# Attention over heads: block-diagonal grids in halves of 64 rows, with fewer and larger strided transfers

## What is computed

```python
fq = jax.nn.elu(q) + 1.0                        # q, k, v: token, 16 heads, 16 numbers
fk = jax.nn.elu(k) + 1.0
kv = jnp.einsum('bhnd,bhne->bnde', fk, v)       # for each token 16 x 16, summed over heads
qkv = jnp.einsum('bhnd,bnde->bhne', fq, kv)
qk = jnp.einsum('bhnd,bnd->bhn', fq, fk.sum(axis=1))
attn = qkv / (qk[..., None] + 1e-06)
```

## Time and profile before

| | |
|---|---|
| median of three runs | 728.25 us (727.19, 728.25, 729.0) |
| profiled execution, span from first to last instruction | 726.3 us |
| TensorE busy | 670.9 us, 92% of the span |
| VectorE, ScalarE, GpSimd busy | 481.1, 420.1, 326.5 us |
| TensorE's granted clock | full in the middle stage, 0.977 in the mean |
| matmuls on keys and on queries | 34.5 and 34.6 us busy, 1024 each |

### The profile page before, as it was taken

How to read it: one execution, slowest core, us unless ns; L and a number is a source line. 1 busy time by engine, 2 the same in 40 slices (tenths; PEclk the granted TensorE clock), 3 DMA queues, 4 the chain that set the end, 5 groups by cost and what they waited for, 6 DMA issues and landing times.

```text
span 726.3 us, 17454 instructions
## 1 busy us (share of the span) xinstructions
PE 670.9 (92%) x6214; PEld 567.6 (78%) x6214; DVE 481.1 (66%) x1332; ACT 420.1 (58%) x841; POOL 326.5 (45%) x493
## 2 busy tenths in 40 slices
PE   7689999998777999999999999999999885999994
PEld 5449999975566788888888888888888663999994
DVE  7856757425688766767777768677676565777751
ACT  5755556502334767676767676766754642766660
POOL 5234563122232453545573664745547563353312
PEclk9879999999999999999999999999999998999998
DMA  8479788404656444544555555555433343567720
GB/s 264 149 241 322 229 270 276 139 29 119 98 99 109 91 66 90 95 87 66 101 86 85 117 84 129 68 108 91 86 73 96 116 132 109 167 215 217 219 93 29
DMA packets 287104, 95.56 MB, mean 132 GB/s; under 512 B 213989, under 2 KB 284737, under 8 KB 287019
## 3 DMA queue, kind: packets, MB, share of 16 engines
q1 hardware_dynamic: 272298, 85.48, 48.9%
q0 software_dynamic: 3840, 8.32, 3.6%
q10 hardware_dynamic: 10880, 0.66, 1.0%
HBM read 65.09 MB, written 29.40 MB: 130 GB/s over the span
## 4 chain that ended last, share of the span: by engine, by line
PE 75%; DVE 8%; issue 6%; ACT 4%; POOL 2%; DMA 2%; SPq 1%; ACTq 1%; POOLq 0%; DVEq 0%
PE bank L1735 68%; PE bank L1744 7%; DMA qkv_rows<-feats 1%; POOL hids L795 1%; SPq L373 1%; ACTq L373 1%; ACT hids L1038 1%; DMA x_all<-in_L_attn_q_x_dram 1%; ACT feats L1001 1%; POOL table L677 1%; ACT feats L999 0%; DVE kv_ L1679 0%; ACT ots L1063 0%; DVE sth L1687 0%; DVE att_ L1576 0%
## 5 line engine op out<-in xcount | busy, mean ns | idle before, releaser
L1735 PE MATMUL bank<-down_w,hids 128*128 128x256 f32 x768 | 105.8, 286 | 1.9 <-POOL hids L795 1.6
L1735 PE MATMUL bank<-hnts,up_w 128*128 128x512 f32 x384 | 104.4, 407 | 0.0
L795 POOL TENSOR_TENSOR hids<-hid,hids 128x512 fp32r<-128x512 f32 x64 | 83.1, 1298 | 41.0 <-ACT hids L1038 40.6
L1735 PEld LDWEIGHTS bank<-down_w,hids 128*128 128x128 f32 x768 | 95.7, 188 | 6.2 <-POOL hids L795 3.4
L1735 PE MATMUL bank<-qkv_w,xnts 128*128 128x256 f32 (+1 forms) x384 | 76.4, 346 | 5.7 <-DVE xnts L1589 4.8
L1735 PEld LDWEIGHTS bank<-hnts,up_w 128*128 128x128 f32 x384 | 67.5, 189 | 11.4
L1735 PEld LDWEIGHTS bank<-qkv_w,xnts 128*128 128x128 f32 x384 | 60.6, 189 | 18.2 <-DVE xnts L1589 7.5
L1035 ACT ACTIVATE hid<-bank,cols 128x512 f32<-128x512 f32 x64 | 44.1, 688 | 45.8 <-PE bank L1735 45.5
L786 POOL TENSOR_SCALAR sth<-sth 128x1 f32<-128x1 f32 x32 | 7.2, 226 | 125.3 <-DVE sth L1601 125.3
L1735 PE MATMUL bank<-a_w,xa_h 128*128 128x256 f32 x256 | 60.2, 379 | 0.0
L1735 PE MATMUL bank<-xa_xt,a_w 128*128 128x256 f32 x384 | 55.1, 294 | 1.4 <-DVE xa_xt L1327 1.4
(11 more groups left out here) (272 smaller groups left out, 1546.9 us busy)
## 6 DMA issues: line engine op xcount, KB each, us to landing
qkv_rows<-feats SPq DMA_DIRECT2D x32, 384.0 KB, 3.4
a_raw<-in_L_ffn_w_dram SPq DMA_DIRECT2D x32, 256.0 KB, 4.1
a_w<-in_L_ffn_w_dram SPq DMA_DIRECT2D x32, 256.0 KB, 3.7
b_raw<-in_L_ffn_w_dram SPq DMA_DIRECT2D x32, 256.0 KB, 3.2
b_w<-in_L_ffn_w_dram SPq DMA_DIRECT2D x32, 256.0 KB, 3.0
mid_rows<-x_all SPq DMA_DIRECT2D x8, 512.0 KB, 2.9
x<-mid_rows SPq DMA_DIRECT2D x32, 128.0 KB, 2.4
values<-qkv_rows SPq DMA_DIRECT2D x32, 128.0 KB, 2.9
```

Source lines behind the costliest of these rows:

```text
L795: pool.tensor_tensor(hids[1][u % 3][:], hid[u % 2][:], f32(hids[0][u % 3][:]), ALU.subtract).then_inc(s_hidl, 1)
L1735: return pe.matmul(dst, left, right, start=start, stop=stop, skip_group_check=True)
```

## The change

The grids of keys and queries become half as wide. Partition `4*(16r+h)+u` of set `s` holds token `8s+2u+r`: the even tokens stand in partitions 0 to 63, the odd ones in 64 to 127, each half block-diagonal over four tokens in 64 columns. Each call of `mm` becomes two with 64 rows and 64 columns, the second half's results in the next bank (KV). All eight banks are now one PSUM tensor, so that one view (`sums`) spans both. Values, keys and queries are loaded by four transfers each of every fourth partition: 12 a tile. For every tile ScalarE's queue issues two of the keys and one of the queries (three for tile 0), SyncE the others. Copy and transpose read the new order. Bank KV holds a half of the sums, so `turn_o` moves to bank TURN, and the router's second turns and counts to bank V, with the waits that go with them.

```diff
+    HALVES, QUADS = 2, 4
+    HALF = P // HALVES
...
-        bank = [ctx.enter_context(nc.psum_tensor(f"bank{i}", [P, 512], F32)) for i in range(8)]
+        banks = ctx.enter_context(nc.psum_tensor("bank", [P, 8, 512], F32))
+        bank = [banks[:, i] for i in range(8)]
...
-            keys = tiles(mid, "keys_", 2, [P, SETS, P])
-            queries = tiles(mid, "queries_", 2, [P, SETS, P])
+            keys = tiles(mid, "keys_", 2, [P, SETS, HALF])
+            queries = tiles(mid, "queries_", 2, [P, SETS, HALF])
+            tile(mid, "below_x", [P, 2, SETS, P])
...
+        sums = banks[:, B_ATT:B_KV + 1, 0:4 * HALF]
...
-        HELPED = 7
+        HELPED = NT
         def keys_by_sp(n):
-            return (4 if n == 0 else 5) if n < HELPED else 8
+            return 2 if n < HELPED else QUADS
         def queries_by_sp(n):
-            return (2 if n == 0 else 6) if n < HELPED else 8
...
-        def issue_keys(engine, n, t):
...
-            i, rows = n % 2, slice(n * P, (n + 1) * P)
-            engine.dma_start(keys[i][t * HEADS:(t + 1) * HEADS, :, t * HD:(t + 1) * HD],
-                             qkv_rows[1, rows, :].rearrange(
-                                 "(s t) (h d) -> t h s d", t=8, h=HEADS)[t]).then_inc(s_kvin[i], 16)
...
-        def issue_queries(engine, n, t):
-            i, rows = n % 2, slice(n * P, (n + 1) * P)
-            engine.dma_start(queries[i][t * HD:(t + 1) * HD, :, t * HEADS:(t + 1) * HEADS],
-                             qkv_rows[0, rows, :].rearrange(
-                                 "(s t) (d h) -> t d s h", t=8, d=HD)[t]).then_inc(s_qin[i], 16)
+            return (1 if n == 0 else 3) if n < HELPED else QUADS
...
+        def of_quad(c, n, u):
...
+            return qkv_rows[c, n * P:(n + 1) * P, :].rearrange("(s u r) (k x) -> u (r k) s x", u=QUADS, r=HALVES, k=16)[u]
...
+        def issue_values(engine, n, u):
+            engine.dma_start(values[n % 2][u::QUADS, :, 0:HD], of_quad(2, n, u)).then_inc(s_kvin[n % 2], 16)
...
+        def issue_keys(engine, n, u):
+            engine.dma_start(keys[n % 2][u::QUADS, :, u * HD:(u + 1) * HD], of_quad(1, n, u)).then_inc(s_kvin[n % 2], 16)
...
+        def issue_queries(engine, n, u):
+            engine.dma_start(queries[n % 2][u::QUADS, :, u * HEADS:(u + 1) * HEADS], of_quad(0, n, u)).then_inc(s_qin[n % 2], 16)
         def set_of(i, j):
...
-                i, rows = n % 2, slice(n * P, (n + 1) * P)
+                i = n % 2
...
-                sp.dma_start(values[i][:, :, 0:HD], qkv_rows[2, rows, :].rearrange(
-                    "(s t) (g e) -> (t g) s e", t=8, g=HEADS)).then_inc(s_kvin[i], 16)
-                for t in range(keys_by_sp(n)):
-                    issue_keys(sp, n, t)
+                for u in range(QUADS):
+                    issue_values(sp, n, u)
+                for u in range(keys_by_sp(n)):
+                    issue_keys(sp, n, u)
             def load_queries(n):
...
-                for t in range(queries_by_sp(n)):
-                    issue_queries(sp, n, t)
+                for u in range(queries_by_sp(n)):
+                    issue_queries(sp, n, u)
             def store_x2(g):
...
-                for t in range(queries_by_sp(n), 8):
-                    issue_queries(act, n, t)
+                for u in range(queries_by_sp(n), QUADS):
+                    issue_queries(act, n, u)
             def help_keys(n):
...
-                for t in range(keys_by_sp(n), 8):
-                    issue_keys(act, n, t)
+                for u in range(keys_by_sp(n), QUADS):
+                    issue_keys(act, n, u)
             def copy_kvt(n):
...
-                act.copy(kvt[:], bank[B_ATT][:].rearrange("p (i c) -> p i c", i=4)).then_inc(s_kvt, 1)
+                act.copy(kvt[:].rearrange("p i (r d u) -> p i r d u", r=HALVES, d=HD),
+                         sums.rearrange("p r (i u d) -> p i r d u", i=4, u=QUADS)).then_inc(s_kvt, 1)
             def gelus(g, m):
...
-                    act.copy(ots[0][n % 2][:], bank[B_KV][:, 0:D]).then_inc(s_o, 1)
+                    act.copy(ots[0][n % 2][:], bank[B_TURN][:, 0:D]).then_inc(s_o, 1)
...
-                    features(n, bank[B_KV])
+                    features(n, bank[B_V])
...
-                dve.tensor_tensor(ots[1][n % 2][:], bank[B_KV][:, 0:D], f32(ots[0][n % 2][:]), ALU.subtract).then_inc(s_ol, 1)
+                dve.tensor_tensor(ots[1][n % 2][:], bank[B_TURN][:, 0:D], f32(ots[0][n % 2][:]), ALU.subtract).then_inc(s_ol, 1)
             def attended(n):
...
-                dve.transpose(att[:], bank[B_ATT][:].rearrange("p (i t h) -> p h i t", i=4, t=8)).then_inc(s_att, 1)
+                dve.transpose(att[:], sums.rearrange("p r (t h) -> p h t r", h=HEADS)).then_inc(s_att, 1)
...
-                    read_counts(routed(s, 2), bank[B_KV])
+                    read_counts(routed(s, 2), bank[B_V])
...
-                pe.wait_ge(s_kvin[n % 2], 16 * 9 * (n // 2 + 1))
+                pe.wait_ge(s_kvin[n % 2], 16 * 2 * QUADS * (n // 2 + 1))
...
-                        last = mm(bank[B_ATT][32 * j:32 * j + 32, i * P:(i + 1) * P], values[n % 2][:, set_of(i, j)],
-                                  keys[n % 2][:, set_of(i, j)], True, True)
+                        for r in range(HALVES):
+                            rows = slice(r * HALF, (r + 1) * HALF)
+                            last = mm(sums[32 * j:32 * j + 32, r, i * HALF:(i + 1) * HALF],
+                                      values[n % 2][rows, set_of(i, j)], keys[n % 2][rows, set_of(i, j)], True, True)
...
-                pe.wait_ge(s_qin[n % 2], 16 * 8 * (n // 2 + 1))
+                pe.wait_ge(s_qin[n % 2], 16 * QUADS * (n // 2 + 1))
...
-                        last = mm(bank[B_ATT][32 * j:32 * j + 32, i * P:(i + 1) * P], kv[:, i, 32 * j:32 * j + 32],
-                                  queries[n % 2][:, set_of(i, j)], True, True)
+                        for r in range(HALVES):
+                            rows = slice(r * HALF, (r + 1) * HALF)
+                            last = mm(sums[32 * j:32 * j + 32, r, i * HALF:(i + 1) * HALF],
+                                      kv[rows, i, 32 * j:32 * j + 32], queries[n % 2][rows, set_of(i, j)], True, True)
...
-                    last = turn(bank[B_KV][:, k * P:(k + 1) * P], on[n % 2][:, k * P:(k + 1) * P])
+                    last = turn(bank[B_TURN][:, k * P:(k + 1) * P], on[n % 2][:, k * P:(k + 1) * P])
...
-            kv_free = None
...
-                    pe.wait_ge(*kv_free)
+                    pe.wait_ge(*turn_free)
...
-                    kv_free = (s_ol, s - 4)
+                    turn_free = (s_ol, s - 4)
...
-                    if kv_free:
-                        pe.wait_ge(*kv_free)
...
-                    kv_free = (s_kv, s - 3)
...
-                    pe.wait_ge(*kv_free)
-                    turned(n, bank[B_KV])
-                    kv_free = (s_bfeat, n + 1)
+                    pe.wait_ge(*v_free)
+                    turned(n, bank[B_V])
+                    v_free = (s_bfeat, n + 1)
...
-                    pe.wait_ge(*kv_free)
-                    count(g, bank[B_KV])
-                    kv_free = (s_bdisp, 9 * g + 1)
+                    pe.wait_ge(*v_free)
+                    count(g, bank[B_V])
+                    v_free = (s_bdisp, 9 * g + 1)
...
-                    pe.wait_ge(*kv_free)
+                    pe.wait_ge(s_att, 4 * NT)
...

```

## The result

| | before | after |
|---|---|---|
| median of nine runs each, us | 729.19 (727.19 to 729.38) | 730.79 (730.32 to 732.34) |
| profiled execution, span, us | 726.3 | 729.9 |
| mean granted clock | 0.977 | 0.966 |

The ratio is 1.0031 (95% interval 1.0022 to 1.0039): slower by 0.3%, where 20 us less were forecast. The medians lie 1.6 us apart and the two profiled spans 3.5 us: the execution profiled before (728.25) is one of the faster of its nine, the one after (731.59) one of the slower. Ratios leave out executions over 1.5% above the fastest of the same kernel. In the page of the changed kernel the chain is as it was, TensorE's; the instructions fetched (q8) have grown from 50 packets of 0.82 MB to 66.

What follows compares the result with a forecast made beforehand. TensorE's stream was taken to bound the middle steps; 16.6 us there and in the last two tiles plus 3.4 in the first six steps made 20.0 off the 726.3 span, 706.3, plus 1.95: 708.3 us, range 702 to 722.

Steps and rivals of the forecast that it cites:

- The blocks: sum_kv and sum_att on TensorE: each block of matmuls takes 0.59 us instead of 1.01, 0.42 less, 0.84 a step.
- Rival 3: TensorE's blocks: doubled matmuls are handed out too slowly, 1.8 us a block, 775 us in total; chance 0.07.
- What ends next: Middle steps: ScalarE's copy of the values, which project needs, leaves 0.30 us spare; gains total 16.6 us.
- the 0.12 taken from 15 steps: Middle steps: part of sum_kv's 0.42 us lost to a new wait of project for the values' copy, leaving 0.72 a step.
- The wait for the choice of expert: Four middle steps where TensorE already waits 0.2 us for VectorE: wait grows to 0.6, all of sum_kv's 0.42 lost.
- ScalarE's issues: Three more transfers a tile on ScalarE's queue from the eighth tile on, covered by the table load: cost taken as 0.
- The first six steps: Steps from 181 to 234 us: fewer issues and shorter sum_att, less turn_o's delay, gain 3.4 us, bounds 0 and 7.
- The five gains of `sum_att`: Early steps: the shorter block on queries saves time five more times, 2.1 us in all.
- `turn_o`'s 0.2 us: Early steps: moved to bank TURN, it comes ahead of qkv in four or five steps, costing 0.9 us.
- The strided copies: ScalarE's copy of kvt reading PSUM at a step of 16 elements: taken as 0, at worst 0.50 us.
- Rival 1: ScalarE becomes the bound through a 0.50 us dearer strided copy or held-up issues: 12 us given back, 720; chance 0.14.
- rival 2: Halves of a column group take turns, or something other than columns sets the round: blocks stay 1.01 us, 727; chance 0.12.

## Why the prediction was wrong, point by point

**The blocks (mis-sized).** "64 recorded matmuls, eight side by side, again 8 rounds" of 0.055 us held for the first four rounds alone (0.238 us); the other four took 0.375 (0.32 with half the columns). A block gave 0.22 us, not 0.42; 10.7 us in 24 steps instead of 20. This is the largest term of the forecast, and it was sized at twice what came. Rival 3 had this mechanism, with its break-even of 16 ns a matmul: the rate was 11.7 ns, in half of the block, so it halved the gain and did not turn it. The row set against it, eight loads and four matmuls within 85 ns, showed the start of a block, where 32 stand ready; nothing in it could show the 33rd. The price set for this rival, 0.026 us a matmul, came from a row whose granted clock reads 0.50; the prediction did not say so. The 25 ns from start to start, which the prediction quoted from the Trainium skill ("TensorE: Matmul & The Clock Gate", section "Wait — 56ns, not 53.3ns?"), are contradicted in both parts of the block.

**What was not there at all: broken blocks.** They cost 3.8 us from tile 6 to tile 30 of the profiled run. Their cause is open. The run with the number of instructions of before (half of the sets, 50 packets fetched) has only two after its first two blocks, 0.58 and 0.19 us, but these first two lose 1.06 and 1.13, more than in the changed kernel (0.66 and 0.73); and the one with transfers to neighbouring partitions has the 66 packets and one broken block. That fetching instructions beside the grids' transfers breaks them is a guess that fits these two in part.

**What ends next (held).** ScalarE's chain keeps its distance from the block, so what is spare decides, and the block's gain was 0.22 us, less than the 0.30 that were spare: in the steps from 303 us on `project` starts as soon after `turn_kv` as before (0.35 us where nothing stands between), and the 0.12 taken from 15 steps did not come. In the four steps with 0.08 spare (256 to 291 us) it starts at 0.50 instead of 0.35: 0.15 lost, of a gain of 0.22, where 0.34 of 0.42 were predicted. The wait for the choice of expert grew from 0.2 to 0.4.

**ScalarE's issues ("Taken: 0").** In the middle this held for ScalarE's chain: they lay under the table load as predicted, and the relu came no later, though they took 0.58 to 0.66 us, not 0.31. What they cost in the total, 0.8 and 1.9 us by two pairs of medians, is not well told from nothing. The late turn of hn, 1.9 us in four steps, no step of the prediction foresaw; it comes with and without these issues, ScalarE's copy ahead of it waits for TensorE's own turn, and its cause is open. "Bytes and pieces of 64 bytes are the same" was true and beside the point: the step of partitions was not weighed.

**The first six steps (wrong sign).** +3.4 was forecast, -5.3 came. The largest part is the first tile: 1.5 us were to be won by fewer issues ahead of its copy of kvt, and tile 1's keys came 3.8 us later. The prediction counted the issues and left out what they wait for. ScalarE's keys of tile 1 wait for that tile's store, and SyncE issued the store 1.5 us later, behind the dearer transfers; so the copy came 1.9 us later instead of sooner, TensorE waited 3.1 us, and the clock fell. The five gains of `sum_att` did not exist: TensorE's next work there waits for VectorE's low part of hn, and that wait grew from 0.36 to 0.55 us. `turn_o`'s 0.2 us cost 0.94 in four or five steps, as said. The clock fell three times, at most 5.6 us, of which idle products gave back 2.8 by tile 5. No step of the prediction asked what fewer busy microseconds in an engine that waits do to its clock, though the stretch was known to be busy 41 of 53 us.

**The strided copies** cost nothing, as taken: the copy of kvt takes 0.587 us before and after. The transpose takes 0.708 instead of 0.704. Rival 1's price did not exist; rival 2's mechanism neither.

**The rest.** After tile 30, 1.05 us were lost. Kernels with the same last stage lie between 185.4 and 187.2 us there (before 185.8, after 186.9), so this is no effect of the change that these runs can show.

The sum, from tile 6 to tile 30: 10.7 from the blocks and 0.3 at `turn_o`, less 3.8 of broken blocks, less 2.0 between `project` and the turn of hn, less 2.4 elsewhere (0.6 in the projection of queries, keys and values with the wait for the choice behind it, 0.6 in the router's logits, 0.5 in its counts, 0.4 ahead of `project`, 0.3 in small ones), is 2.8, as measured; 2.8 - 5.3 - 1.05 is -3.5.

What stays open: why moving `turn_o` costs 2.4 us in the total where its early steps lose 0.94; what breaks the blocks and what delays the turn of hn, 5.7 us together; why the two kernels with another order of tokens or rows spread over 8 and 12 us; what throws the clock at 201 us where no idle piece is long; and how the clock and the later transfers share the early loss, since each of the two runs (idle products, neighbouring partitions) takes away more than half.

## What to carry to other kernels

A rate read off the first few instructions after a wait is the rate of a filled queue: before doubling the number of small matmuls, find a stretch that is longer than the queue, or measure one. A shape of transfer has its own price per issue, even for the same bytes and pieces, and what stands behind the issues in the order of an engine waits with them, the first copy of kvt here: ask of an issue also what it waits for itself. And where an engine waits already, making it faster gives nothing and can cost its clock (with half of the blocks' work tile 6 came 3.3 us later still): look at the granted clock of the stretches in which it is not the bound.

## What was not expected of the hardware

- Small matmuls with their weight loads start 7.5 ns apart for the first 32 of a block and 11.7 ns after that; with half the columns 5 ns and still about 10.
- A transfer to every fourth partition is issued in 0.61 to 0.67 us, whether of 16 or 32 partitions; to 32 neighbouring ones in 0.49 to 0.57, to 16 in 0.45 to 0.53.
- The granted clock fell to 0.50 after two of four idle pieces of 1.18 to 1.84 us (after 1.50 and 1.84, not after 1.18 and 1.78) beside blocks of 0.79 us. It did not fall beside four pieces of 0.96 to 1.61 us and blocks of 1.01 us, and it fell once where no piece was longer than 0.73 us.
- ScalarE reads PSUM with a step of 16 elements as fast as in a row (0.587 us for 512).
